# A LoRA residual kernel: one level of a seven-product matrix scheme against two levels, with another order of VectorE's queue

## The chip, the cores and the metric

The kernel runs on one core of a Trainium2 chip. The metric is the device time of one execution in microseconds (us), the median of three runs; what follows also reads one execution that the hardware profiler recorded.

## The reference, cut to what matters

Each of the two steps adds to x what a low-rank pair makes of it; the second also adds the product with a full matrix. x is (8, 512, 2048), W is (2048, 2048), every rank is 16, and all of it is float32.

```python
# step 1: A, B picked per batch element by itok_B_3_7
x = x + einsum('bnr,bor->bno', einsum('bni,bri->bnr', x, B[ids0]), A[ids0])
# step 2: lora_A, lora_B picked per batch element by itok_B_0_15
x = x + (einsum('bsi,io->bso', x, W)
         + einsum('bsr,bro->bso', einsum('bsi,bir->bsr', x, lora_A[ids1]), lora_B[ids1]))
```

## The kernel before, in words

The output is held transposed. The residual is put into the weights (W plus the identity, in the code `eye`), so that one matrix product gives nearly all, and the low-rank parts join it as one more matmul for each output tile: `in_mm` finds the values (`lr_ps`), `p_mm` finds the first step's A times W (`p_ps`), `join` makes `val`, `lr_out` adds `lr_w` times `val`.

A float32 operand is split into a rounded part and a rest: ScalarE (ACT) casts the rounded part (`w_hi` L555, `b_hi` L566), VectorE (DVE) subtracts it (`w_lo` L708, `b_lo` L721), and TensorE (PE) runs three matmuls for each tile: hi by hi, hi by lo, lo by hi (L1024).

The matrix product is done for pairs of batch elements by a seven-product scheme on 2x2 blocks of 1024 (`P1, P2, P6, P7, P4, P3, P5`), so 7 block products take the place of 8. A pair p has 7 products, each product 8 units, and a unit n is 4 output tiles by 2 chunks of 128 by 3 matmuls: 24 matmuls of 512 columns. The four pairs make 224 units. The sums of W's blocks are made once (`w_add` L694) and kept in HBM (`w_sum`), those of x are made in place (`t1` to `t4`).

Each engine has its own queue, written out by hand in the order of the units: in iteration n ACT and DVE split the operands of unit n + 1 into one of two buffers, PE works on unit n, and DVE adds the accumulator banks of ended tiles to what is kept (`add` L760 to L769, `add_last` L776 and L777). Five banks rotate (`BANKS`), and PE waits for the one of five tiles ago before it opens a new one:

```python
                    if j == 0 and k >= BANKS:
                        pe.wait_ge(*bank_free(k - BANKS))
```

A tile stays open over four units, and the adds of a group of four tiles are spread over the next ones. The SP queue issues the loads of W and x and the stores of W's sums, the POOL queue issues the loads picked by index, those of `lrw` and all stores of outputs.

Of the kernel before, what the change touches and what calls it, by code (L numbers as in the profile page):

```python
# [22 lines left out]
P1, P2, P6, P7, P4, P3, P5 = range(7)  # L24
PRODUCTS, UNITS = 7, 8

X11, X12, X21, X22 = range(4)

S2, S3 = range(2)

A11, A12, A21, A22 = range(4)

P_PRODUCTS = (P1, P2, P7, P4)


def lora_residual_program(nc, xT, ids0, ids1, A0n, B0, W, A1, B1, yT):
# [3 lines left out]
    N = xT.shape[3]  # L40
    D = C * P
    HC = C // 2
    HD = D // 2
    PAIRS = NB // 2
    LAST = PAIRS * PRODUCTS * UNITS
    BANKS, RAWS, STAGES = 5, 4, 4

    def at(n):
        return n // (PRODUCTS * UNITS), n // UNITS % PRODUCTS, n % UNITS

    def unit(p, o, u):
        return (p * PRODUCTS + o) * UNITS + u

    def diagonal(p, o, u):

        return (o in (P1, P4, P5) or (p, o) == (0, P6)) and u // 4 == u % 4 // 2

    def two_blocks(p, o):

        return o in (P3, P5) or (p, o) == (0, P6)  # L60
# [3 lines left out]
    raw_of, raw_plan = {}, []  # L64
    for n in range(LAST):
        p, o, u = at(n)
        raw_of[n] = len(raw_plan)
        raw_plan.append(n)
        if two_blocks(p, o) or (p, o) == (0, P1):
            raw_plan.append(n)  # L70

    def main_raw(n):
        return raw_of[n] % RAWS

    def second_raw(n):
        return (raw_of[n] + 1) % RAWS


    s3_stores, stores = {}, [0] * RAWS
    for u in range(UNITS):  # L80
        r = raw_of[u] + 1
        stores[r % RAWS] += 1
        s3_stores[r] = stores[r % RAWS]

    presums = [n for n in range(LAST) if two_blocks(*at(n)[:2]) or diagonal(*at(n))]
    begun = [n for n in presums if two_blocks(*at(n)[:2]) and diagonal(*at(n))]


    stage_plan = []
    for p in range(PAIRS):  # L90
        stage_plan += [("fix", p, q) for q in range(2 * UNITS)] if p == 1 else []
        for kind, half in (("c11", 0), ("c21", 1)):
            for g in range(2):
                stage_plan += [(kind, p, 4 * g + t) for t in range(4)]
                stage_plan += [("pst", half, g)] if p == 0 else []
    stage_at = {use: s for s, use in enumerate(stage_plan)}


    lr_plan = [(0, 1, 0, unit(0, P3, 2)), (0, 1, 1, unit(0, P3, 5)), (0, 0, 0, unit(0, P5, 5)),
               (0, 0, 1, unit(1, P1, 2))]  # L100
    for p in range(1, PAIRS):
        lr_plan += [(p, 0, 0, unit(p, P1, 5)), (p, 0, 1, unit(p, P7, 6)), (p, 1, 0, unit(p, P3, 2)),
                    (p, 1, 1, unit(p, P3, 5))]
    lr_index = {use[:3]: i for i, use in enumerate(lr_plan)}
    lr_split_at = {use[3]: i for i, use in enumerate(lr_plan)}
    lr_load_at = {use[3] - (2 if i == 4 or use[1:3] == (1, 0) else 3): i for i, use in enumerate(lr_plan)}


    join_at = {unit(p, P2, 2) if p else unit(0, P4, 1): 2 * p for p in range(PAIRS)}
    join_at |= {unit(p, P3, 2): 2 * p + 1 for p in range(PAIRS)}  # L110
    j_split_at = {unit(p, P2, 0) if p else unit(0, P4, 0): 2 * p for p in range(PAIRS)}
# [7 lines left out]
    stk_at |= {unit(p, P6, 6): (2 * p + 1, 0) for p in range(PAIRS)}  # L119
    stk_at |= {unit(p, P7, 5): (2 * p + 1, 1) for p in range(PAIRS)}  # L120

    def slot_due(n):

        if n < UNITS:
            if n + 1 < 4:
                return 0, n + 1
# [15 lines left out]
    def finds_p(n):  # L142
        return n // UNITS in P_PRODUCTS

# [944 lines left out]
```

## Time and profile before

| | |
|---|---|
| median of 3 runs | 1402.17 us (1401.36 to 1405.29) |
| the profiled execution's own time | 1402.34 us |
| its span, first to last instruction | 1400.7 us |
| PE busy | 1367.2 us (98%), 6016 matmuls |
| DVE busy | 810.2 us (58%) |
| ACT busy | 405.9 us (29%) |
| POOL busy | 165.0 us (12%) |
| DMA | 261.81 MB, mean 187 GB/s |

How to read it: busy is the time in which an engine had at least one instruction running, issues of transfers not counted. The profiled execution is a run like the others, and its own time is 1.6 us above its span, so that a sum made against the span needs 1.6 us to be a time.

### The profile page before, as it was taken

Reading aid. Unit: us, or ns where it says so; the run is one execution under the profiler, and the core shown is the slowest. Engines: PE = TensorE matmul, PEld = TensorE weight load, DVE = VectorE, ACT = ScalarE, POOL = GpSimd, SP = SyncE. Lnnn points to the kernel's source line nnn. Section 1 sums busy time; section 2 is a strip of 40 time slices with the busy share of each in tenths; the row PEclk is TensorE's granted clock in tenths of the full one; section 3 lists DMA queues with packets and bytes.
Section 4 is the critical chain, followed back from the end, with each engine's and each line's share of the span. In section 5 each row is a group of like instructions: output and inputs, shape, how many; then the busy total and the mean of one; then the engine's idle time right before and its main releaser. Section 6 shows DMA issues by size and latency. Waiting matters only on the chain.

```text
span 1400.7 us, 15653 instructions
## 1 busy us (share of the span) xinstructions
PE 1367.2 (98%) x6016; PEld 1129.2 (81%) x6016; DVE 810.2 (58%) x941; ACT 405.9 (29%) x462; POOL 165.0 (12%) x317
## 2 busy tenths in 40 slices
PE   5999999999999999999999999999999999999997
PEld 4888888888878888888887888888887888888886
DVE  3455855357776455646775555555766445554675
ACT  2332222223234223322332323232322422232230
POOL 3200100111123010012011010012012001001202
PEclk8999999999999999999999999999999999999999
DMA  8864843458887343357684252446785334234755
GB/s 303 310 225 134 299 158 113 153 186 280 294 280 240 122 136 120 129 195 246 236 289 146 86 173 96 151 151 213 256 297 187 99 120 135 91 91 133 223 201 180
DMA packets 76778, 261.81 MB, mean 187 GB/s; under 512 B 12176, under 2 KB 12176, under 8 KB 76576
## 3 DMA queue, kind: packets, MB, share of 16 engines
q1 hardware_dynamic: 57600, 205.55, 43.5%
q0 software_dynamic: 19104, 55.27, 11.7%
q8 instruction: 48, 0.79, 0.2%
q14 instruction: 26, 0.21, 0.0%
HBM read 213.52 MB, written 48.30 MB: 187 GB/s over the span
## 4 chain that ended last, share of the span: by engine, by line
PE 85%; DVE 5%; DMA 5%; ACT 2%; issue 2%; POOL 0%; POOLq 0%; SPq 0%; ACTq 0%; DVEq 0%
PE y_ps L1024 76%; PE lr_ps L955 4%; PE p_ps L997 3%; DMA w_raw<-in_W 2%; PE y_ps L976 2%; ACT w_hi L555 2%; DVE w_lo L708 1%; DVE w_raw L694 1%; DVE b_lo L721 1%; DMA w_raw<-w_sum 1%; DVE u L776 1%; DMA stage_all<-lrw 0%; DMA u<-in_A0n 0%; DVE u L777 0%; DVE val L835 0%
## 5 line engine op out<-in xcount | busy, mean ns | idle before, releaser
L1024 PE MATMUL y_ps<-b_hi,w_hi 128*128 128x512 f32 x1792 | 699.3, 390 | 15.3 <-DVE w_lo L708 8.8
L1024 PE MATMUL y_ps<-b_lo,w_hi 128*128 128x512 f32 x1792 | 698.6, 390 | 0.0
L1024 PE MATMUL y_ps<-b_hi,w_lo 128*128 128x512 f32 x1792 | 698.4, 390 | 0.0
L708 DVE TENSOR_TENSOR w_lo<-w_raw,w_hi 128x1024 fp32r<-128x1024 f32 x216 | 264.6, 1225 | 460.9 <-ACT w_hi L555 460.9
L555 ACT CAST w_hi<-w_raw 128x1024 fp32r<-128x1024 f32 x216 | 227.6, 1054 | 879.5 <-PE y_ps L1024 474.9
L1024 PEld LDWEIGHTS y_ps<-b_hi,w_hi 128*128 128x128 f32 x1792 | 337.3, 188 | 86.6 <-DVE w_lo L708 8.8
L1024 PEld LDWEIGHTS y_ps<-b_hi,w_lo 128*128 128x128 f32 x1792 | 337.2, 188 | 70.2
L1024 PEld LDWEIGHTS y_ps<-b_lo,w_hi 128*128 128x128 f32 x1792 | 337.3, 188 | 70.1
L721 DVE TENSOR_TENSOR b_lo<-x_raw,b_hi 128x1024 fp32r<-128x1024 f32 x112 | 136.5, 1219 | 0.0
L566 ACT CAST b_hi<-x_raw 128x1024 fp32r<-128x1024 f32 x112 | 117.5, 1049 | 2.4 <-DMA x_raw<-in_xT 2.4
L694 DVE TENSOR_TENSOR w_raw<-w_raw 128x1024 f32<-128x1024 f32 x64 | 78.1, 1221 | 19.5 <-DMA w_raw<-in_W 11.6
L377 POOL DMA_DIRECT2D out_y<-stage_all x64 | 34.9, 546 | 413.9 <-DVE stage_all L760 377.9
L760 DVE TENSOR_TENSOR stage_all<-y_ps,u 128x512 f32<-128x512 f32 x64 | 43.1, 688 | 20.8 <-PE y_ps L976 16.9
L955 PE MATMUL lr_ps<-b_hi,in_stk 128*128 128x512 f32 x128 | 50.4, 394 | 0.0
L955 PE MATMUL lr_ps<-b_lo,in_stk 128*128 128x512 f32 x128 | 50.3, 393 | 0.0
L381 POOL DMA_DIRECT2D out_y<-u x32 | 17.6, 548 | 260.1 <-DVE u L776 259.5
L769 DVE TENSOR_TENSOR u<-y_ps,u 128x512 f32<-128x512 f32 x64 | 41.1, 685 | 7.4 <-PE y_ps L1024 5.0
L976 PE MATMUL y_ps<-val,lr_w 128*128 128x512 f32 x112 | 44.0, 393 | 1.3 <-DVE val L835 1.1
L327 POOL DMA_DIRECT2D in_raw<-in_B x8 | 4.5, 563 | 307.6 <-issue 307.6
L341 POOL DMA_DIRECT2D lr_raw<-lrw x64 | 31.4, 497 | 76.1 <-DVE lr_w L817 68.6
L997 PE MATMUL p_ps<-w_hi,a_hi 128*128 128x512 f32 x64 | 26.0, 407 | 8.2 <-DVE a_lo L784 8.2
L955 PEld LDWEIGHTS lr_ps<-b_hi,in_stk 128*128 128x128 f32 x128 | 24.5, 191 | 5.2
(81 smaller groups left out, 605.8 us busy)
## 6 DMA issues: line engine op xcount, KB each, us to landing
w_raw<-in_W SPq DMA_DIRECT2D x208, 512.0 KB, 3.8
w_raw<-w_sum SPq DMA_DIRECT2D x96, 512.0 KB, 3.6
x_raw<-in_xT SPq DMA_DIRECT2D x64, 512.0 KB, 5.4
out_y<-u POOLq DMA_DIRECT2D x64, 256.0 KB, 6.4
out_y<-stage_all POOLq DMA_DIRECT2D x64, 256.0 KB, 3.4
lr_raw<-lrw POOLq DMA_DIRECT2D x64, 128.0 KB, 4.0
w_sum<-w_raw SPq DMA_DIRECT2D x8, 512.0 KB, 6.2
c_kept<-stage_all POOLq DMA_DIRECT2D x16, 256.0 KB, 3.2
```

Source lines behind the costliest of these rows:

```text
L377: pool.dma_start(dst, stage[s % STAGES][:, :]).then_inc(stage_stored[s % STAGES], 16)
L555: act.copy(w_hi[n % 2][:, :, :], w_tile(n)[:, :, :]).then_inc(w_hi_done, 1)
L566: act.copy(b_hi[:, 2 * j:2 * j + 2, :], x_raw[i][:, 2 * j:2 * j + 2, :]).then_inc(x_hi_done, 1)
L694: last = dve.tensor_tensor(raw[:, :, :], w_raw[main_raw(n)][:, :, :], w_raw[r % RAWS][:, :, :], ALU.subtract if o == P3 else ALU.add)
L708: dve.tensor_tensor(w_lo[n % 2][:, :, :], w_tile(n)[:, :, :], w_hi[n % 2][:, :, :].bitcast(F32), ALU.subtract).then_inc(w_ready, 1)
L721: dve.tensor_tensor(b_lo[:, 2 * j:2 * j + 2, :], x_raw[i][:, 2 * j:2 * j + 2, :], b_hi[:, 2 * j:2 * j + 2, :].bitcast(F32), ALU.subtract). ...
L760: dve.tensor_tensor(stage[s % STAGES][:, :], bank[:, :], (u2 if o == P2 else u3)[:, m, :], ALU.add).then_inc(added, 1)
L769: dve.tensor_tensor(u2[:, m, :], bank[:, :], u2[:, m, :], ALU.add).then_inc(added, 1)
L955: last = pe.matmul(lr_ps[:, :], cols, x[:, c, :], start=(first and c == 0 and x is b_hi), stop=(half == 1 and c == HC - 1 and x is b_lo))
L976: return pe.matmul(out[:, :], lr_w[i % 2][:, m * P:(m + 1) * P], val[b][:, :], start=start, stop=True)
L997: last = pe.matmul(p_ps[:, :], a0[:, 2 * j + c, :], w[n % 2][:, c, :], start=(j == 0 and c == 0 and k == 0), stop=(j == 3 and c == 1 and k ...
L1024: last = pe.matmul(bank[:, :], w[n % 2][:, c, t * P:(t + 1) * P], x[:, 2 * j + c, :], start=(j == 0 and c == 0 and w is w_hi and x is b_hi ...
```

## The change

The scheme is applied twice. Four batch elements (a "quad" k, two of them) are worked on together, an outer scheme of seven products `mo` (`M1, M2, M6, M7, M4, M3, M5`) on blocks of 1024, and inside each an inner scheme of seven products `po` (`Q1, Q2, Q6, Q5, Q7, Q3, Q4`) on blocks of 512. A quad has 49 products of 2 units each (`UNITS = 14` units for each mo), a unit is 2 output tiles by 4 chunks by 3 matmuls: again 24 matmuls of 512 columns. There are 196 units.

The inner products Q1, Q6, Q7 and Q4 (`CHAIN`) accumulate one on top of the other in four banks. The other three (Q2, Q5, Q3) go through a ring of two banks, `r_ps`. DVE adds every product to one or two targets as `ADDS` says; in M1 and M5 ACT copies the first of each target. The sums of operands: `t1` to `t4` (x) and, in the first quad alone, `s1` to `s4` (W) at the inner level, 128x2048 elements each; `xq` and `wq` at the outer level, from two operands, of which the second comes through a ring of three tiles `tmp` of 512 KB (`TMPS = 3`); `t3p` and `s3p`, whose two operands both come through `tmp` and whose result is stored to HBM from there. Outer partial results are kept in `u2` and in `stage`, stored and loaded again (`u3`). The second quad loads W's 49 operands ready-made. In it, tiles whose low-rank part was not known in time are loaded, seeded into a bank by ACT, given a matmul, and copied out (`fixes`, 48 units of M1 to M3), and eight further ones get theirs in `fin`.

Units and what falls in them (u is the unit within an outer product): Q1 u 0, 1; Q2 u 2, 3; Q6 u 4, 5; Q5 u 6, 7; Q7 u 8, 9; Q3 u 10, 11; Q4 u 12, 13. `s3p` (M1 of the first quad) and `t3p` (M2 of both) have one sum in each of u 5 to 12. The 8 gathers of one `a0` or `a1` tile also go through `tmp`.

The diff, cut to its core:

```diff
+CHAIN = (Q1, Q6, Q7, Q4)
+ADDS = {Q1: ((C11, True),), Q2: ((C11, False),), Q6: ((C12, True),), Q5: ((C12, False), (C22, True)),
+        Q7: ((C22, False),), Q3: ((C12, False),), Q4: ((C21, True),)}
-    BANKS, RAWS, STAGES = 5, 4, 4
+    LAST = QUADS * PRODUCTS * 2
+    TMPS = 3
...
+    def early_sums(n):
+        if u == 0 and x_worked(mo):
+            out.append(("xq", k, mo, 1))
+        if u == 4:
+            out.append(("t1", k, mo))
+        if u == 5 and k == 0:
+            out.append(("s1", mo))
+    def late_sums(n):
+            if u == 8 and x_worked(nmo):
+                out.append(("xq", nk, nmo, 0))
...
+        if u == 1:
+            out.append(("t2", k, mo))
+        if u == 2:
+            out.append(("t4", k, mo))
+        if k == 0:
+            if u == 1:
+                out.append(("s2", mo))
+            if u == 3:
+                out.append(("s4", mo))
+            if mo == M1 and 5 <= u < 13:
+                out.append(("s3p", *divmod(u - 5, 2)))
+        if mo == M2 and 5 <= u < 13:
+            out.append(("t3p", k, (C11, C12, C22, C21)[(u - 5) // 2], (u - 5) % 2))
...
+        # POOL
+            def load_tmp(e):
+                if e >= TMPS:
+                    pool.wait_ge(*tmp_free(tmp_plan[e - TMPS]))
...
+            def store_kept(kind, *key):
+                s, _ = tmp_stores[kind + "a", *key]
+                pool.wait_ge(kept_summed, kept_no[kind, *key])
...
+                    if kind in ("s3pb", "t3pb"):
+                        store_kept(kind[:3], *key)
+                        after = [e - 1, e]
+                    for f in after:
+                        if f + TMPS < len(tmp_plan):
+                            load_tmp(f + TMPS)
...
+        # ACT
+            def w_split(n):
+                q, h = divmod(n, 2)
+                if n >= 2:
+                    wait(unit_free(n - 2))
+                act.wait_ge(*w_is_there(q, h))
+                act.copy(w_hi[:, h, :, :], wq[w_tile(q)][:, h, :, :]).then_inc(w_hi_done, 1)
...
+        # DVE
+            for n in range(LAST + 2):
+                sums(early_sums(n))
+                if n + 1 < LAST:
+                    w_split(n + 1)
+                if n // 2 + 1 < LAST // 2:
+                    x_split(n // 2 + 1, n % 2)
+                for q, t, count, c, first in evicts(n, 0):
+                    if not by_act(q, first):
+                        evict(q, t, count, c, first)
...
+                for q, t, count, c, first in evicts(n, 1):
+                    if not by_act(q, first):
+                        evict(q, t, count, c, first)
+                if finish(n):
+                    fin(*finish(n))
+                sums(late_sums(n))
...
+                for key in a_splits(n):
+                    a_split(*key)
...
+        # PE
+                    if po in CHAIN:
+                        out = ps[:, t, :]
+                        if q:
+                            last_q = q - 7 + Q4 if po == Q1 else 7 * (q // 7) + CHAIN[CHAIN.index(po) - 1]
+                            pe.wait_ge(*a_free(last_q, h))
                     else:
+                        r = r_at["tile", q, t]
+                        out = r_ps[r % 2]
+                        if r >= 2:
+                            for pair in r_free(r - 2):
+                                pe.wait_ge(*pair)
...
+                    if n in fixes:
+                        fix(n, t % 2)
+                    if low:
+                        fin(*low, 1 - t % 2)
```

Here `evicts(n, 0)` names what is added of unit n - 1 (both banks of a chained product, the second tile of a ring product), and `evicts(n, 1)` the first tile of unit n, for ring products alone. `r_free` is the end of the adds that read the ring's bank two tiles earlier; `unit_free(n - 2)` is the end of unit n - 2 on PE; `tmp_free` is the end of the sum that used the tile, or, for a tile stored from, the landing of its store. The loads and stores of `tmp` are all issued by POOL, one after the other. In `fin` of the second quad DVE makes two sums of 128x1024, PE two matmuls, DVE two adds, PE two matmuls that wait for these adds, and DVE two adds.

## Rows read from the trace of the kernel before

**Rows 1.** The page's head: busy time of PE and DVE, the slices, the transfers.
```profile
PE 1367.2 (98%) x6016; PEld 1129.2 (81%) x6016; DVE 810.2 (58%) x941; ACT 405.9 (29%) x462; POOL 165.0 (12%) x317
PE   5999999999999999999999999999999999999997
PEclk8999999999999999999999999999999999999999
DMA packets 76778, 261.81 MB, mean 187 GB/s; under 512 B 12176, under 2 KB 12176, under 8 KB 76576
```
**Rows 2.** The page's chain of work that ended last, shares of the span by engine.
```profile
PE 85%; DVE 5%; DMA 5%; ACT 2%; issue 2%; POOL 0%; POOLq 0%; SPq 0%; ACTq 0%; DVEq 0%
```
**Rows 3.** Groups of instructions by line and shape: busy us, mean ns; idle before.
```profile
L1024 PE MATMUL y_ps<-b_hi,w_hi 128*128 128x512 f32 x1792 | 699.3, 390 | 15.3 <-DVE w_lo L708 8.8 <-DVE u L777 6.4
...
L708 DVE TENSOR_TENSOR w_lo<-w_raw,w_hi 128x1024 fp32r<-128x1024 f32 x216 | 264.6, 1225 | 460.9 <-ACT w_hi L555 460.9
L555 ACT CAST w_hi<-w_raw 128x1024 fp32r<-128x1024 f32 x216 | 227.6, 1054 | 879.5 <-PE y_ps L1024 474.9 <-PE p_ps L997 134.2 <-DVE w_raw L703 133.2
...
L760 DVE TENSOR_TENSOR stage_all<-y_ps,u 128x512 f32<-128x512 f32 x64 | 43.1, 688 | 20.8 <-PE y_ps L976 16.9 <-PE y_ps L1024 2.6
...
L573 ACT COPY u<-y_ps 128x512 f32<-128x512 f32 x32 | 18.7, 587 | 21.6 <-PE y_ps L1024 21.6
```
**Rows 4.** Timeline, 700 to 706 us: start, duration, engine, line, operation.
```profile
700.32 0.39 PE L1024 MATMUL y_ps<-b_hi,w_hi 128*128 128x512 f32 x1
...
702.71 1.05 ACT L555 CAST w_hi<-w_raw 128x1024 fp32r<-128x1024 f32 x1 [4.39 <-DVE w_raw L694]
...
703.79 1.23 DVE L708 TENSOR_TENSOR w_lo<-w_raw,w_hi 128x1024 fp32r<-128x1024 f32 x1 [1.17 <-ACT w_hi L555]
...
704.63 0.39 PE L1024 MATMUL y_ps<-b_hi,w_hi 128*128 128x512 f32 x1
...
704.94 0.68 DVE L776 TENSOR_TENSOR u<-y_ps,u 128x512 f32<-128x512 f32 x1
...
705.54 0.68 DVE L777 TENSOR_TENSOR u<-y_ps,u 128x512 f32<-128x512 f32 x1
```
**Rows 5.** Timeline, 58 to 60.5 us: weight loads of 128-column matmuls, a unit's end.
```profile
58.25 0.19 PEld L1005 LDWEIGHTS j_ps<-lr_w,a_lo 128*128 128x128 f32 x1
...
58.58 0.19 PEld L1005 LDWEIGHTS j_ps<-lr_w,a_lo 128*128 128x128 f32 x1
...
60.19 0.40 PE L1024 MATMUL y_ps<-b_hi,w_hi 128*128 128x512 f32 x1
...
60.39 1.05 ACT L555 CAST w_hi<-w_raw 128x1024 fp32r<-128x1024 f32 x1 [6.87 <-PE p_ps L997]
```
**Rows 6.** The tile w_sum's transfers of 512 KB, from issue to landing.
```profile
DMA to landing us min/median/max: 3.0/3.9/9.0
```
**Rows 7.** DMA issues, 0 to 70 us: count, KB each, median us to landing.
```profile
DMA packets 6237, 21.46 MB, mean 307 GB/s; under 512 B 1136, under 2 KB 1136, under 8 KB 6105
...
w_raw<-in_W SPq DMA_DIRECT2D x17, 512.0 KB, 5.9
...
w_sum<-w_raw SPq DMA_DIRECT2D x7, 512.0 KB, 5.5
```
**Rows 8.** Timeline of POOL, first and last of the 8 gathers of A.
```profile
9.10 0.59 POOL L389 DMA_DIRECT2D u<-in_A0n  x1 [6.25 <-issue]
...
17.54 0.54 POOL L389 DMA_DIRECT2D u<-in_A0n  x1 [0.59 <-issue]
```
**Rows 9.** The first matmul, and the first matmul behind the gathers, in the timeline.
```profile
8.84 0.80 PE L1024 MATMUL y_ps<-b_hi,w_hi 128*128 128x512 f32 x1 [8.84 <-DVE w_lo L708]
...
24.67 0.79 PE L997 MATMUL p_ps<-w_hi,a_hi 128*128 128x512 f32 x1 [8.20 <-DVE a_lo L784]
```
**Rows 10.** Windows: PE, PEld, DVE, ACT, POOL busy, PEclk, DMA share, GB/s.
```profile
16.00:24.60 8.60, 0.47 (x3) 0.05 (x1) 1.28 (x7) 0.85 (x3) 3.77 (x7) 0.72 0.86 300
...
24.60:30.00 5.40, 5.33 (x13) 4.17 (x14) 3.54 (x7) 2.83 (x5) 2.15 (x4) 0.50 0.66 187
```

More of the change, by code:

```diff
@@ L85, in lora_residual_program @@
[L85 to L95, printed above, removed]
@@ L106, in lora_residual_program @@
[L106 to L111, printed above, removed]
-    j_split_at |= {unit(p, P3, 0): 2 * p + 1 for p in range(PAIRS)}
-    j_load_at = {unit(p, P1, 3) if p else unit(0, P7, 4): 2 * p for p in range(PAIRS)}
@@ new lines, in product, with by_act @@
+    def product(q):
+        return q // 49, q // 7 % 7, q % 7
+    def by_act(q, first):
+        return first and product(q)[1] in (M1, M5)
+    fixes = {}
+    for mo, pair, own, quarters in ((M1, 0, 0, (0, 1)), (M2, 0, 0, (2, 3)), (M6, 1, 0, (0, 1)), (M7, 1, 0, (2, 3)),
+                                    (M4, 0, 1, (0, 1)), (M3, 0, 1, (2, 3))):
+        for i, u in enumerate((3, 4, 6, 7, 9, 10, 12, 13)):
+            fixes[unit(1, mo, u)] = (batch(own, pair, i // 2 % 2), 4 * quarters[i // 4] + 2 * (i % 2))
@@ new lines, in lora_residual_program, with use_tmp @@
+    lr_split_of = {i: n for n, uses in lr_split_at.items() for i in uses}
+    lr_mms = {}
+    for n in range(LAST + 1):
+        if n in fixes:
+            for t in range(2):
+                lr_mms["fix", n, t] = len(lr_mms) + 1
+        end = finish(n)
+        if end and end[0]:
+            for which in (1, 0):
+                for t in range(2):
+                    lr_mms["fin", end[1], end[2], which, t] = len(lr_mms) + 1
+    tmp_plan, tmp_when = [], []
+    def use_tmp(n, late, *key):
+        tmp_plan.append(key)
+        tmp_when.append((n, late))
@@ new lines, in lora_residual_program @@
+    g_at = {unit(0, M1, 5): 0, unit(0, M2, 5): 1}
+    p_no = {key: i + 1 for i, key in enumerate((mo, po) for mo in P_OF for po in P_Q)}
+    r_plan = []
+    for n in range(LAST):
+        if n % UNITS // 2 not in CHAIN:
+            r_plan += [("tile", n // 2, 2 * (n % 2)), ("tile", n // 2, 2 * (n % 2) + 1)]
+        if n in g_at:
+            r_plan.append(("g", g_at[n]))
+        if n in join_at:
+            r_plan.append(("join", *join_at[n]))
+    r_at = {key: r for r, key in enumerate(r_plan)}
@@ new lines, in lora_residual_program, with bank_of @@
+        p_reads, p_read = {}, {}
+        adds = copies = 0
+        for mo, po in p_no:
+            p_reads[mo, po] = {Q1: (0, 1), Q2: (0,)}.get(po, (1,))
+            if po == Q1 and mo in (M1, M4):
+                copies += 1
+                p_read[mo, po] = p_copied, copies
+            else:
+                adds += len(p_reads[mo, po])
+                p_read[mo, po] = p_added, adds
+        def bank_of(q, t, count):
+            if q % 7 in CHAIN:
+                return ps[:, t:t + count, :]
+            return r_ps[r_at["tile", q, t] % 2]
@@ L545, in _, with wait @@
+            for s in range(TMPS):
+                sp.wait_ge(tmp_stored[s], 16 * sum(stored_from(key) for key in tmp_plan[s::TMPS]))
+            for s in range(2):
+                sp.wait_ge(fix_stored[s], 16 * (len(fixes) // 2))
+            for c in range(4):
+                for h in range(2):
+                    sp.wait_ge(u2_stored[c][h], 16 * QUADS)
         @block.scalar
         def _(act):
+            def wait(pairs):
+                for pair in pairs:
+                    act.wait_ge(*pair)
@@ L943, in _ @@
+                if n in val_split_at:
+                    val_split(*val_split_at[n])
         @block.tensor
         def _(pe):
[L945 to L957 removed]
```

1951 lines of the change are left out of this document (1166 added, 785 removed).

## The prediction, made before the changed kernel ran

> **What bounds the kernel now.** I read the page's head first. PE is busy 1367.2 us of 1400.7, and from the second slice on every slice but the last is at nine tenths or more [rows 1]. The chain that ended last is PE for 85% [rows 2]. The groups then say that nothing starves it: 15.3 us of idle stand before 1792 of its matmuls, 8.8 of them at the start, while DVE waited 460.9 us for ACT's casts and those 474.9 us for PE [rows 3]. So the kernel is 6016 matmuls at their pitch. The timeline has that pitch: from 700.32 to 704.63 us is 19 matmuls, 0.227 us each [rows 4]; a unit of 24 is 5.44 us, a tile of 12 is 2.72. Times 6016 this is 1364 us.
>
> **What the change takes from PE.** The main product falls from 224 to 196 units, 5376 to 4704 matmuls. I count beside them 256 of in_mm, 128 of lr_out, 24 of join: 5112 matmuls at 0.227 = 1159 us. p_mm becomes 384 matmuls of 256 columns. No row has these. Below they can't beat 128 columns, whose weight loads come every 0.11 us (three from 58.25 to 58.58) [rows 5], above they don't exceed 0.227: 42 to 87 us. Half the columns lie near the lower end, I take 0.12, 46 us. With 48 matmuls of g at 0.11 (5 us) PE's work is 1210 us, 157 less than now. If all else were hidden, that would be the gain.
>
> **What it puts on DVE.** Issue to issue, a 128x1024 operation takes 1.15 us (703.79 to 704.94) and a 128x512 one from a bank 0.60 (704.94 to 705.54) [rows 4]; by this slope 1024 from a bank is 1.14 and the new 2048-element sums 2.2 (bounds: 2.1 to two of 1.15). For one outer product: 28 splits, 32 us; eight double-bank adds and sixteen single ones, 9 + 10; t1 to t4, 9; in the first quad s1 to s4, 9 more. That is 60 us, 69 in the first quad, before the outer sums, and 14 units are 76 us of PE. The outer sums (24 xq, 12 wq, 24 kept sums, 16 fins) add about 170 us in all. DVE goes to some 1100 us busy. It is no bound by its sum, but it now stands in line with PE at four places.
>
> **First place, the ring of two banks.** The second tile of a ring product's second unit needs the bank of that product's tile two before, which DVE adds in this same unit and behind both splits. From the unit's start: ACT begins 0.20 us later (60.19 to 60.39) [rows 5], casts 1.05, DVE follows at 1.29, splits w (1.15) and x (1.15), so the add starts at 3.58 and is complete 0.68 later: PE gets the bank at 4.3, and wanted it at 2.72. 1.6 us are lost after Q3, 2.2 after Q5 where two adds read each bank. In Q2 DVE arrives late, since t2 and t4 (and s2) stand in units 1 and 2. Walking DVE's queue by these durations through the 14 units: t2 ends 6.9 us into unit 1, so DVE comes 1.5 us late to unit 2, ends it at 7.8 and is 2.1 late to unit 3, whose second tile then waits 2.4. The waits come to 0.3 + 2.4 (Q2), 0.6 + 1.6 (Q5, half regained in front) and 1.6 (Q3) = 6.4 us for an outer product, 8.6 in the first quad, where s2 makes the first of them 2.4. ACT's seeds and copies of the fix units (0.59 each [rows 3], two in front of the cast) add about 1 in the second quad. p_mm and in_mm give DVE time and take some off. I carry for the seven, in order M1, M2, M6, M7, M4, M3, M5: 5, 5, 14, 9, 8, 10, 12 in the first quad (M6, M3 and M5 also have xq and wq at their edges) and 7, 4, 9, 8, 8, 8, 8 in the second. Sum 115. Without the cover of those extra matmuls it would be some 20 more.
>
> **In the last M5** fin's second pair of matmuls waits for DVE's adds of the first: splits to 3.6, adds of banks to 4.8, two sums to 7.2, two adds to 8.5, two matmuls to about 8.8, where the unit wants 6.3. Eight units at 2.6 are 21 us.
>
> **Second place, the ring of three tiles.** A kept sum reads two tiles; the next but three load may be issued only when the store from the first has landed, and DVE waits for it in its one queue, with the split of the unit after next behind. One turn is the sum 1.22, the store, the load, and 0.2 for the handover. A 512 KB transfer of w_sum lands in 3.9 us median, 3.0 at least [rows 6]: a turn is 9.2 us (7.4 at least), PE's own pace 5.44 to 8.6. Where two operands of xq or wq come between (u 8 to 12 of M2; u 8, 10, 12 in the second quad), another sum and load are in the turn: 9.2 + 1.3 + 3.9 = 14.4. From u 5 to u 12: M1 seven turns, 64 us, for 48 that PE would take (with its p_mm, in_mm and ring waits), +16. M2 2 x 9.2 + 5 x 14.4 = 90, +42. M2 of the second quad 4 x 9.2 + 3 x 14.4 = 80 for 49, +31. Sum 89. At the least landing it is near 45.
>
> **Third place, the gathers through the same ring.** Eight gathers take POOL 9.0 us to issue (9.10 to 18.1) [rows 8], and the tile lands some 4 later. In M7 at u 12 two such tiles stand ahead of a0's split, the second issued only after xq's tile is free, about 6.5 us into the unit: 6.5 + 13 + the difference and both splits 3.5 = 23, and the split for the next product but one comes 2.4 after, where PE wants it at 10.9: +15. At M5's start, with one, +11. Handovers of xq and wq tiles at the edges of M6, M4 and M5: +15, a guess between 0 and 30. Sum 41.
>
> **Ends.** The first matmul comes at 8.84 now [rows 9]; two 1 MB operands and four more identity adds make that about 12.5, and p_mm still waits for the gathers, as it does now (24.67 [rows 9]), after which the clock is at half, 1.2 GHz, for some us (0.50 from 24.6 to 30.0) [rows 10]. I take 20 us over the work for the start, and 8 for the last fin and its stores.
>
> **Sum.** 1210 + 115 + 21 + 89 + 41 + 20 + 8 = 1504 us of span, + 1.6 outside it = 1505. The profiled execution (1402.34) is the median (1402.17) within 0.2 us, so this stands against either: 7% slower. 0.3% is about what a measurement of this kernel can tell from no change.
>
> **The rivals.**
> Transfers slow down under their own load. I count 399 MB where there were 262: the 173 tiles of the ring 91, x 59, W 81, stores of W's sums 44, other stores and the fixes 124. In M2 some 44 MB move. In the first 70 us of the trace, at 307 GB/s, 512 KB loads took 5.9 us and stores 5.5 [rows 7]. Turns are then 12.8 and 20.0 us, the third sum 180 instead of 89, the total 1596. For it: M2 needs 300 GB/s at my own forecast. Against: the load is this dense only in M1 and M2.
>
> The clock falls. After 8.2 us of idle [rows 9] the clock went to half, 1.2 GHz (0.50) [rows 10]. If the waits of M1's and M2's kept sums do this each time, a unit's 24 matmuls take up to twice 5.44 us, about one short turn, and where p_mm or a bank wait comes on top it runs over: some 2 us on each of 24 units, +45 in all, 1550. Against: most of my waits are 1.6 to 5 us; PEclk is 9 in every slice after the first [rows 1], though PE has hardly a wait there. The Trainium skill (TensorE: Matmul & The Clock Gate, "HAM oscillation") describes a kernel that waits for a transfer between groups of matmuls and runs each group at the low clock. By that rule it would be 1550; no row here has such a pattern.
>
> The three-tile ring does not hold DVE, because landings are near 3 us and POOL has issued ahead. Then the kept sums and handovers cost nothing, only bank waits, gathers and ends remain: 1505 - 89 - 15 = 1401, no change. To be faster, the gathers' tiles must also have come early (26 less), 1375. It decides from a turn under about 6.9 us, PE's mean pace there, that is two landings under 5.5 together; the least of the rows gives 6.0 [rows 6].
>
> The change does what its matmul count says, all else hidden: 1240. Against it stands the bank wait, made of three durations that hardly vary.
>
> **Chances.** The forecast, 1450 to 1560: 0.5. Slow transfers or low clock, 1560 to 1660: 0.22. Ring mostly hidden, 1406 to 1450: 0.12; fully, within 0.3% of 1402: 0.03; faster with the gathers hidden too: 0.10; all hidden: 0.03. So faster 0.13, same 0.03, slower 0.84. The range 1390 to 1600 leaves about 0.11 below it (half of the cases near 1375 and all hidden, with a little) and 0.08 above; the slower cases alone hold 1430 to 1600.
>
> **What the profile of the changed kernel would show.** PE's busy near 1210 to 1240 us, DVE's near 1100. PE idle before ring tiles released by DVE's adds, 1.5 to 2.5 us, some 40 times. In M2 (about 150 to 290 us, and again about 140 us long in the second quad) units spaced 9 and 14 us, DVE idle at the kept sums, released by transfers into tmp; the clock there says which rival. One hole of about 15 us at the end of M7. The prediction is wrong if the tmp transfers are not what DVE waits for in M2, if the landing there is far from 3.9, or if the matmul pitch is not 0.227. DMA should total 400 MB.

## The result, and the profile after

The changed kernel takes 1705.34 us (median of 4 runs, 1698.28 to 1710.05) where the one before took 1401.76: the ratio is 1.2156, its 95% interval 1.2101 to 1.2212. It is 21.6% slower; 7% was forecast, and the time lies above the range. The profiled execution took 1698.28 us, its span is 1696.6.

The page of the changed kernel, the lines that answer to [rows 1] and [rows 2]:

```profile
PE 1328.5 (78%) x5544; PEld 1057.9 (62%) x5544; DVE 1114.0 (66%) x1105; ACT 570.4 (34%) x720; POOL 346.6 (20%) x603
...
PE   5879673469996998966897897457898888888895
...
PEclk9989896779998999987998998778999999999998
...
DMA packets 106324, 401.25 MB, mean 236 GB/s; under 512 B 15092, under 2 KB 15092, under 8 KB 99716
...
PE 26%; issue 23%; DMA 20%; DVE 20%; POOL 4%; ACT 3%; POOLq 1%; DVEq 0%; ACTq 0%
```

The reader is to see that the work is as counted (5544 matmuls, 401 MB, DVE 1114 us busy) and that the kernel has no bound of its own any more. PE had 85% of the chain that ended last [rows 2] and has 26%; transfers and DVE have 20% each. "issue", time for which the profile shows no wait, has 23% where it had 2%. Part of it hides waits for transfers: one such piece runs from 233.78 to 242.77 us, and DVE waited for a load of the three-tile ring in 8.83 us of the same stretch (its line stands below). Two valleys stand in PE's row, deepest in the seventh and eighth slice and in the 26th and 27th: M2 of either quad. The granted clock has its 6 and three of its five 7s there too.

Groups of the changed kernel, as in [rows 3], and its transfers from issue to landing:

```profile
L1636 PE MATMUL ps<-b_hi,w_hi 128*128 128x512 f32 x1568 | 650.8, 415 | 258.0 <-DVE stage L1380 108.9
...
L1349 DVE TENSOR_TENSOR w_lo<-wq,w_hi 128x1024 fp32r<-128x1024 f32 x196 | 239.8, 1224 | 317.9 <-ACT w_hi L1069 317.2
...
L1310 DVE TENSOR_TENSOR xq<-xq 128x2048 f32<-128x2048 f32 x56 | 127.8, 2283 | 0.0
L1161 ACT COPY ps<-wq 128x512 f32<-128x512 f32 x96 | 56.7, 590 | 195.9 <-DMA wq<-c_kept 190.4
...
tmp<-t_kept POOLq DMA_DIRECT2D x48, 512.0 KB, 6.5
wq<-c_kept POOLq DMA_DIRECT2D x48, 512.0 KB, 7.1
out_y<-wq POOLq DMA_DIRECT2D x48, 512.0 KB, 4.7
```

258 us of idle stand before PE's first matmuls of a chunk, where 15.3 stood [rows 3], most of it (109 + 66 us in the view of waits below) released by DVE's adds. ACT's seeds of the fix units waited 190.4 us for their loads. The loads of the three-tile ring land in 6.5 us, not in the 3.9 of [rows 6].

From the starts of the splits of w (one a unit, L1349) the length of each outer product can be read. Beside the changed kernel stand four of the runs below. "Forecast" is worked out from the prediction's terms, to about 3 us: PE's work in that product and the waits that it put there. The first M1 has none, since the start of the kernel lies in it, and the second M5 is left out.

| product | forecast | changed | adds first | no kept x sums | no fix copies | five out |
|---|---|---|---|---|---|---|
| first M1 | | 134.7 | 135.6 | 134.8 | 135.5 | 98.4 |
| first M2 | 142 | 174.6 | 179.1 | 113.6 | 173.6 | 112.2 |
| first M6 | 90 | 114.5 | 107.3 | 113.3 | 115.4 | 104.8 |
| first M7 | 108 | 109.4 | 98.5 | 109.9 | 109.3 | 92.2 |
| first M4 | 96 | 94.1 | 88.5 | 94.0 | 94.3 | 90.6 |
| first M3 | 94 | 105.0 | 100.3 | 105.3 | 105.5 | 99.3 |
| first M5 | 111 | 124.6 | 117.8 | 123.7 | 124.6 | 112.5 |
| second M1 | 94 | 114.6 | 110.9 | 115.8 | 104.7 | 106.0 |
| second M2 | 122 | 158.5 | 156.3 | 108.7 | 153.9 | 86.2 |
| second M6 | 89 | 106.4 | 99.5 | 104.6 | 97.5 | 93.8 |
| second M7 | 95 | 109.0 | 99.5 | 108.3 | 95.3 | 87.0 |
| second M4 | 88 | 104.8 | 95.2 | 101.5 | 87.0 | 81.3 |
| second M3 | 95 | 104.0 | 98.1 | 105.5 | 92.7 | 87.0 |

### The profile page after: what moved, and what is told of

Read it like the earlier page. It is cut to its first block, busy times and chain, and to the rows that moved or that the text cites. A ratio compares the mean times of both kernels' runs of the same rounds, so it can differ in the third digit from the quotient of the medians.

```text
span 1696.6 us, 16085 instructions
## 1 busy us (share of the span) xinstructions
PE 1328.5 (78%) x5544; PEld 1057.9 (62%) x5544; DVE 1114.0 (66%) x1105; ACT 570.4 (34%) x720; POOL 346.6 (20%) x603
## 4 chain that ended last, share of the span: by engine, by line
PE 26%; issue 23%; DMA 20%; DVE 20%; POOL 4%; ACT 3%; POOLq 1%; DVEq 0%; ACTq 0%
PE ps L1636 22%; DMA wq<-c_kept 5%; DVE w_lo L1349 4%; DVE xq L1310 3%; DMA tmp<-in_W 3%; DVE stage L1380 3%; DVE b_lo L1355 3%; DMA tmp<-in_xT 2%; DMA t_kept<-tmp 2%; ACT w_hi L1069 2%; DMA tmp<-t_kept 2%; POOL tmp L790 2%; DMA out_y<-wq 1%; PE ps L1603 1%; PE ps L1566 1%
## 5 line engine op out<-in xcount | busy, mean ns | idle before, releaser
L1636 PE MATMUL ps<-b_hi,w_hi 128*128 128x512 f32 x1568 | 650.8, 415 | 258.0 <-DVE stage L1380 108.9
L1636 PE MATMUL ps<-b_lo,w_hi 128*128 128x512 f32 x1568 | 638.6, 407 | 0.0
L1636 PE MATMUL ps<-b_hi,w_lo 128*128 128x512 f32 x1568 | 636.4, 406 | 0.0
L1636 PEld LDWEIGHTS ps<-b_hi,w_hi 128*128 128x128 f32 x1568 | 312.5, 199 | 357.0 <-issue 143.0
L1349 DVE TENSOR_TENSOR w_lo<-wq,w_hi 128x1024 fp32r<-128x1024 f32 x196 | 239.8, 1224 | 317.9 <-ACT w_hi L1069 317.2
L1069 ACT CAST w_hi<-wq 128x1024 fp32r<-128x1024 f32 x196 | 205.7, 1049 | 533.7 <-PE ps L1636 379.2
L1636 PEld LDWEIGHTS ps<-b_hi,w_lo 128*128 128x128 f32 x1568 | 310.9, 198 | 69.7
L1636 PEld LDWEIGHTS ps<-b_lo,w_hi 128*128 128x128 f32 x1568 | 312.6, 199 | 63.8
L1355 DVE TENSOR_TENSOR b_lo<-xq,b_hi 128x1024 fp32r<-128x1024 f32 x196 | 238.9, 1219 | 4.1 <-ACT b_hi L1075 3.8
L1075 ACT CAST b_hi<-xq 128x1024 fp32r<-128x1024 f32 x196 | 205.3, 1048 | 88.1 <-DVE xq L1295 63.8
L1310 DVE TENSOR_TENSOR xq<-xq 128x2048 f32<-128x2048 f32 x56 | 127.8, 2283 | 0.0
L1161 ACT COPY ps<-wq 128x512 f32<-128x512 f32 x96 | 56.7, 590 | 195.9 <-DMA wq<-c_kept 190.4
L1318 DVE TENSOR_TENSOR tmp<-tmp 128x1024 f32<-128x1024 f32 x24 | 29.4, 1225 | 119.7 <-DMA tmp<-in_xT 82.7
L1531 PE MATMUL ps<-val,lr_w 128*128 128x512 f32 x128 | 56.9, 458 | 61.3 <-ACT ps L1161 50.4
L1380 DVE TENSOR_TENSOR u<-ps,u 128x512 f32<-128x512 f32 (+1 forms) x124 | 100.3, 839 | 2.3 <-PE ps L1636 2.1
L872 POOL DMA_DIRECT2D out_y<-wq x48 | 34.9, 727 | 210.2 <-ACT wq L1165 190.6
```

The lines of the kernel that those rows point to most:

```text
L1069: act.copy(w_hi[:, h, :, :], wq[w_tile(q)][:, h, :, :]).then_inc(w_hi_done, 1)
L1075: act.copy(b_hi[:, 2 * (q % 2) + j, :, :], xq[x_use(q)[0]][:, j, :, :]).then_inc(x_hi_done, 1)
L1161: act.copy(p_ps, fix_tile[fix_no[n] % 2][:, t, :]).then_inc(seeded, 1)
L1310: dve.tensor_tensor(xq[dst][:, :, :, :], xq[a][:, :, :, :], xq[b][:, :, :, :], ALU.subtract).then_inc(x_summed, 1)
L1349: dve.tensor_tensor(w_lo[:, h, :, :], wq[w_tile(q)][:, h, :, :], w_hi[:, h, :, :].bitcast(F32), ALU.subtract).then_inc(w_ready, 1)
L1355: dve.tensor_tensor(b_lo[:, slot, :, :], xq[x_use(q)[0]][:, j, :, :], b_hi[:, slot, :, :].bitcast(F32), ALU.subtract).then_inc(x_ready, 1)
```

## The experiments

Sixteen kernels ran. Each comes from the changed kernel by the edit shown; differences are to its 1705.34 us. Its own four runs spread over 12 us, and most of the others have two runs, so a single difference under 10 us says little. Some of the edits leave out needed work or read other data than they should; they show what a place costs and are no kernels to use.

### The place of the adds in DVE's queue

```diff
             for n in range(LAST + 2):
                 sums(early_sums(n))
+                for q, t, count, c, first in evicts(n, 0):
+                    if not by_act(q, first):
+                        evict(q, t, count, c, first)
                 if n + 1 < LAST:
                     w_split(n + 1)
                 if n // 2 + 1 < LAST // 2:
                     x_split(n // 2 + 1, n % 2)
-                for q, t, count, c, first in evicts(n, 0):
-                    if not by_act(q, first):
-                        evict(q, t, count, c, first)
```

> DVE adds the banks of the ended unit ahead of the splits, as the kernel's two-level form would without the second half of the change; all else as changed (1705 us). If the ring of two banks costs what I worked out (1.6 to 2.4 us at the second tile of each of 42 ring products, where nothing else holds the unit), the banks are free before PE asks and some 40 to 75 us go: 1630 to 1665 us. If the adds' place is nothing because DVE waits for transfers anyway, it stays within 10 us of 1705. If the later splits starve PE instead, it is over 1715.

1624.82 us (ratio to the kernel before 1.1619, interval 1.1564 to 1.1673): 80 us less, where 40 to 75 were expected. PE's waits for DVE's adds halve; the same rows of the view of waits (us in total, times, longest), in the changed kernel and in this run:

```profile
PE ps L1636 <- DVE stage L1380: 108.9, 37, 18.0
PE ps L1636 <- DVE u L1380: 66.0, 26, 10.5
...
PE ps L1636 <- DVE stage L1380: 48.4, 9, 15.1
PE ps L1636 <- DVE u L1380: 42.1, 11, 15.4
```

63 waits became 20, where the forecast had some 40; 59 of the 63 stood in the second unit of a ring product. Against it, PE's waits for w_lo grew from 7.1 to 62.5 us, nearly all in the first quad. One wait can be seen in the last units of the first M6. In the changed kernel, the timeline of PE and of DVE:

```profile
423.39 0.39 PE L1636 MATMUL ps<-b_hi,w_lo 128*128 128x512 f32 x1
424.99 0.50 PE L1636 MATMUL ps<-b_hi,w_hi 128*128 128x512 f32 x1 [1.21 <-DVE u L1380]
```

```profile
421.97 1.23 DVE L1349 TENSOR_TENSOR w_lo<-wq,w_hi 128x1024 fp32r<-128x1024 f32 x1 [1.34 <-ACT w_hi L1069]
423.11 1.22 DVE L1355 TENSOR_TENSOR b_lo<-xq,b_hi 128x1024 fp32r<-128x1024 f32 x1
424.25 1.28 DVE L1380 TENSOR_TENSOR u<-ps,u 128x512 f32<-128x512 f32 x2
```

DVE waits for ACT's cast, splits w and x, and adds the bank at 424.25; PE asked for it at 423.6 and opens the tile at 424.99. The same unit with the adds first (it runs at other times there):

```profile
421.34 0.69 DVE L1380 TENSOR_TENSOR u<-ps,u 128x512 f32<-128x512 f32 x1 [1.35 <-PE ps L1636]
...
422.43 1.23 DVE L1349 TENSOR_TENSOR w_lo<-wq,w_hi 128x1024 fp32r<-128x1024 f32 x1 [0.40 <-ACT w_hi L1069]
```

The add falls into the time in which DVE waits for the cast, starts 3 us earlier with respect to the unit, and pushes the split back by nothing. In that order PE has no wait in this stretch.

### The kept sums and their ring of three tiles

Left out the sums of x:

```diff
-        if mo == M2 and 5 <= u < 13:
-            out.append(("t3p", k, (C11, C12, C22, C21)[(u - 5) // 2], (u - 5) % 2))
...
-                        pool.wait_ge(*kept_store("t3p", k, c, j))
-                        src = t3_kept[c, :, j, :, :]
+                        src = xT[batch(k, 1, c % 2), c // 2, :, j, :, :]
```

> Leaves out the 16 kept sums of x in M2 of both quads with their 32 loads and 16 stores; what reads their result loads a block of x of the same size instead. If the ring of three tiles is what M2 waits for (174.6 and 158.5 us between its first splits and the next product's), M2 falls to about 120 and 112 and the total by 95 to 110 us, to about 1600. If M2's length comes from something else (clock, all transfers together), it falls by less than 50.

1586.56 us, 119 less, somewhat more than the 95 to 110 expected: M2 from 174.6 and 158.5 to 113.6 and 108.7, and no more than 3.3 us in any other product. The edit takes away 32 loads and 16 stores as well as the sums, so it gives the price of the place and not of one link in it.

The same for W in the first M1:

```diff
-            if mo == M1 and 5 <= u < 13:
-                out.append(("s3p", *divmod(u - 5, 2)))
...
-                        pool.wait_ge(*kept_store("s3p", c, h))
-                        src = w_kept_at(M7, c)[:, h, :, :]
+                        src = W[4 * (c // 2) + c % 2, :, h, :, :]
```

> Leaves out the 8 kept sums of W in M1 of the first quad; what reads their result loads a block of W instead. By the same ring theory M1's units from u 7 on (9 to 14 us) fall to 6 to 9 and the product from 134.7 us to about 108: total 1675 to 1685. If M1 is long from its start (gathers, clock, first loads), under 10 us go.

1671.19 us, 34 less (its two runs lie 12 us apart), M1 from 134.7 to 109.5. One turn in M2 shows where the time is. The timeline of the changed kernel, DVE and POOL (L1318 is the kept sum, L1246 the sum of wq with its second operand from the ring):

```profile
241.26 1.23 DVE L1318 TENSOR_TENSOR tmp<-tmp 128x1024 f32<-128x1024 f32 x1 [8.83 <-DMA tmp<-in_xT]
...
242.78 0.54 POOL L866 DMA_DIRECT2D t_kept<-tmp  x1 [9.00 <-DVE tmp L1318]
...
245.97 0.53 POOL L790 DMA_DIRECT2D tmp<-w_ops  x1 [2.66 <-DMA t_kept<-tmp]
...
252.82 1.23 DVE L1246 TENSOR_TENSOR wq<-wq,tmp 128x1024 f32<-128x1024 f32 x1 [5.80 <-DMA tmp<-w_ops]
254.08 0.90 DVE L1224 TENSOR_TENSOR wq<-wq,eye 128x128 f32<-128x128 f32 x4
...
255.28 0.55 POOL L790 DMA_DIRECT2D tmp<-in_xT  x1 [7.52 <-DVE wq L1224]
...
261.44 1.23 DVE L1318 TENSOR_TENSOR tmp<-tmp 128x1024 f32<-128x1024 f32 x1 [6.46 <-DMA tmp<-in_xT]
```

From sum to sum it is 20.2 us: the sum and its handover 1.5, the store 3.2, a load 6.8, the sum of wq with the identity 2.5, the next load 6.2. These are the prediction's links; it had 14.4, with 3.9 for each landing and 1.3 for the sum of wq. The two loads took 5.2 us more than that, the sum with the identity 1.2 more, and the store 0.7 less.

The landing goes with what else is under way. Over the changed kernel, 512 KB loads took 4.0 us in the median where no other transfer of 256 KB or more was in flight at their issue (42 loads), 5.8 with two of them (108), 6.8 with three (124) and 9.1 with five (31). In the kernel before it was 3.5 with none (136 loads) and 6.2 with three (41).

Next, the loads of both operands in 256 of their 1024 columns:

```diff
+                cols = 256 if kind in ("t3pa", "t3pb") else 1024
-                pool.dma_start(tmp[slot][:, :, :].rearrange("p s n -> p (s n)"), ...
+                pool.dma_start(tmp[slot][:, :, :].rearrange("p s n -> p (s n)")[:, 0:cols], ...
```

> The two operands of each kept sum of x are loaded in 256 of 1024 columns (the rest is what the tile held); the sum, the store and the order of the ring are as before. If a turn of the ring is the landing of its serial loads, the operand's 6.2 us falls to 3 or so and M2's long units from 15 to 20 us to 12 to 17, the total by 30 to 50 us. If the landing is a wait for POOL's issue or a latency that does not go with size, under 15 us.

1676.51 us, 29 less, just under the 30 to 50 expected; M2 fell by 12.6 and 8.5 us. A quarter of the bytes did not bring a quarter of the landing. The issues in 222 to 310 us of that run, and behind them the same loads in the same window of the changed kernel:

```profile
tmp<-in_xT POOLq DMA_DIRECT2D x10, 128.0 KB, 5.2
...
tmp<-w POOLq DMA_DIRECT2D x2, 512.0 KB, 6.3
...
tmp<-in_xT POOLq DMA_DIRECT2D x9, 512.0 KB, 6.3
```

Last, the second quad's kept sums of x moved from M2 to M1:

```diff
-        if mo == M2 and 5 <= u < 13:
+        if mo == (M1 if k else M2) and 5 <= u < 13:
             out.append(("t3p", ...
```

> In the second quad the kept sums of x stand in M1's units 5 to 12, where no xq sum stands between them, instead of M2's. If a turn with two operands of xq in it costs two landings in a row and one without costs one, M2 of the second quad falls from 158.5 to about 112 and M1 rises from 114.6 to 130 to 140: total 20 to 35 us less. If only the amount of transfers counts, the total stays within 10 us of 1705.

1683.40 us, 22 less. Second M2 158.5 to 111.1, second M1 114.6 to 149.0: a turn without an operand of xq in it is shorter, by less than I had expected, since M1's eight sums cost 34 us and not 20.

### The fix units

Left out the loads into the two tiles, ACT's seeds and copies, and PE's wait for them; POOL moves the tile from HBM to HBM instead:

```diff
         # PE
-                pe.wait_ge(seeded, 2 * fix_no[n] + t + 1)
-                lr_out(b, m + t, p_ps, False)
+                lr_out(b, m + t, p_ps, True)
         # POOL
...
-                pool.dma_start(fix_tile[f % 2], c_kept[b * C + m:b * C + m + 2, :, :].rearrange("m p n -> p m n")
-                               ).then_inc(fix_loaded[f % 2], 16)
+                pool.dma_start(yT[b * C + m:b * C + m + 2, :, :], c_kept[b * C + m:b * C + m + 2, :, :]
+                               ).then_inc(fix_stored[f % 2], 16)
         # ACT: seed and fixed_copy left out; POOL: store_fix left out
```

> Leaves out the low-rank part of the 96 tiles of the fix units: no seed, no copy out by ACT, no load into a tile; POOL moves the tile from HBM to HBM, PE's matmul runs into its bank without waiting. If the fix units' load, seed, copy and store chain is the term that I mis-sized (second quad's products 9 to 20 us over my walk), 60 to 90 us go: 1615 to 1645. If, as I forecast, ACT's copies add only about 1 us a product, 5 to 15 us go.

1629.27 us, 76 less, all in the second quad: M1 to M3 lose 5 to 18 us each. The prediction had about 1 us a product for it. Is it that ACT's casts stand behind seeds which wait?

```diff
         # ACT, each iteration
-                if n - 1 in fixes:
-                    fixed_copy(n - 1, 1)
-                if n in fixes:
-                    seed(n, 0)
                 if 0 <= n < LAST:
                     if n + 1 < LAST:
                         w_split(n + 1)
...
+                if n - 1 in fixes:
+                    fixed_copy(n - 1, 1)
                 if n in fixes:
+                    seed(n, 0)
                     fixed_copy(n, 0)
                     seed(n, 1)
```

> ACT casts the next unit's operands ahead of the fix units' copy out and seed, instead of behind them. Leaving the whole chain out gave 76 us. If most of it is that the casts stand behind a seed that waits for its load, 25 to 60 us go: 1645 to 1680. If it is the loads' and stores' own turn (two tiles, a store and a load in a row for every three units), PE waits for the seed instead and under 15 us go.

1718.74 us, 13 more, where 25 to 60 less were expected if that were so. PE now waits for the seed instead; the waits of PE in that run:

```profile
PE ps L1530 <- ACT ps L1161: 92.5, 32, 9.5
```

In the changed kernel that row is 50.4 us. So I tried the turn of the two tiles:

```diff
-                pool.dma_start(fix_tile[f % 2], c_kept[b * C + m:b * C + m + 2, :, :].rearrange("m p n -> p m n")
+                pool.dma_start(fix_tile[f % 2][:, :, 0:128],
+                               c_kept[b * C + m:b * C + m + 2, :, 0:128].rearrange("m p n -> p m n")
```

> The fix tiles are loaded in 128 of each 512 columns (the rest is what the tile held); seeds, copies and stores as before. If the turn of the two fix tiles (copy, store 4.7 us, load 7.1 us, seed, matmul) is the 76 us, a load that lands in 3 to 4 us takes 25 to 60 us off: 1645 to 1680. If ACT's copies are the cost, under 10.

1678.89 us, 26 less. Here too a 128 KB load landed in 5.0 us where the full one took 7.1:

```profile
wq<-c_kept POOLq DMA_DIRECT2D x48, 128.0 KB, 5.0
```

Two microseconds off a landing gave 26 us back. So the loads are in the chain, which is the turn of two tiles (copy, store, load, seed, matmul), one for every three units. That this turn makes up the whole 76 us is read from the timeline and not shown by a run. There is one more link in it, POOL's queue: the load of a tile is issued behind the store of the other one. POOL and ACT in the second M6 of the changed kernel (L872 stores, L810 loads, L1161 seeds):

```profile
1205.36 0.73 POOL L872 DMA_DIRECT2D out_y<-wq  x1 [6.36 <-ACT wq L1165]
1214.76 0.72 POOL L872 DMA_DIRECT2D out_y<-wq  x1 [8.68 <-ACT wq L1165]
1215.47 0.71 POOL L810 DMA_DIRECT2D wq<-c_kept  x1
...
1222.58 0.59 ACT L1161 COPY ps<-wq 128x512 f32<-128x512 f32 x1 [6.22 <-DMA wq<-c_kept]
```

The first store landed 5.1 us after its issue, at 1210.5; the load into its tile went out at 1215.47, 5.0 us later. The seed of that load started at 1222.58, after ACT had waited 6.22 us with the next cast behind it. An earlier place for these loads in POOL's queue was not tried. From load to load a tile turned in 18 to 22 us once this product was under way, where three units of PE's work are 16.3.

### The gathers

```diff
-                for b in range(NB):
-                    a = id1(b) if which else id0(b)
-                    pool.dma_start(tmp[slot]...[:, b, :, :],
-                                   src[bass.ds(a, 1), :, kh * HC:(kh + 1) * HC, :].rearrange("a p c r -> (a p) c r")
-                                   ).then_inc(tmp_loaded[slot], 16)
+                pool.dma_start(tmp[slot][:, :, :].rearrange("p s n -> p (s n)")
+                               .rearrange("p (b m) -> p b m", b=NB),
+                               src[0:NB, :, kh * HC:(kh + 1) * HC, :].rearrange("a p c r -> p a (c r)")
+                               ).then_inc(tmp_loaded[slot], 128)
```

> The 8 gathers by index of each a0 or a1 tile become one load of 512 KB of the first eight adapters (so the adapters are not the ones asked for). If POOL's issue of 8 gathers in the three-tile ring is what holds M7's last unit (21.9 us) and M5's first two (15.9 and 19.9), these fall to 7 to 10 and the total by 30 to 40 us, to about 1670. If the wait there is the ring's order alone, under 10 us.

1687.88 us, 17 less, half of what was expected. M7's last unit went from 21.9 to 18.1 us, M5's second from 19.9 to 12.9; against it, the first split of w came at 15.8 us instead of 12.3. In M7 the second tile's one load is issued at 528.2 and its sum starts at 536.49, in the timeline of this run:

```profile
528.20 0.91 POOL L728 DMA_DIRECT2D tmp<-in_A0n  x1 [1.76 <-DVE xq L1293]
...
536.49 1.23 DVE L1416 TENSOR_TENSOR tmp<-tmp 128x1024 f32<-128x1024 f32 x1 [6.41 <-DMA tmp<-in_A0n]
```

The issue of eight gathers is only a part of that hole. By this reading the rest is the ring's order, which lets the load go only behind the sums of xq, and some 8 us to the sum.

### PE's own pace and the clock

Left out one of the three matmuls of each tile and chunk, hi by lo:

```diff
-                        for i, (w, b) in enumerate(((w_hi, b_hi), (w_hi, b_lo), (w_lo, b_hi))):
+                        for i, (w, b) in enumerate(((w_hi, b_hi), (w_lo, b_hi))):
...
```

> Leaves out the matmul hi by lo of every chunk, 1568 of the 4704 of the product (356 us of PE at full clock); the splits stay as they are. If PE's pace, half clock included, is what the changed kernel's units last, about 350 us go: 1350 or less. If the units are set by DVE's queue, the transfers and the two rings, less than half of it goes: 1500 to 1600, and M2 stays within 10 us of 174.6 and 158.5 us.

1646.67 us: 356 us of matmuls at full clock were taken away, PE's busy time fell by 267.5 us (the granted clock was 0.83 over that run, 0.91 over the changed kernel), and the kernel lost 59. M2 is 180.2 and 160.3 us long, no shorter than before. That answers the rival of the clock for M2. M2 of the first quad, one window of the changed kernel (columns as in [rows 10]), and PE's timeline at the end of one of its waits:

```profile
147.00:322.00 175.00, 109.92 (x504) 90.19 (x502) 95.83 (x95) 33.72 (x37) 39.48 (x72) 0.83 0.72 244
```

```profile
267.41 0.77 PE L1636 MATMUL ps<-b_hi,w_hi 128*128 128x512 f32 x1 [18.01 <-DVE stage L1380]
...
270.11 0.46 PE L1636 MATMUL ps<-b_hi,w_hi 128*128 128x512 f32 x1
```

The granted clock was 0.83 there, about a third of the stretch at 1.2 GHz. The Trainium skill (TensorE: Matmul & The Clock Gate, "HAM oscillation") describes how such waits for a transfer lower the clock, and the trace agrees. But it costs little here: the low stretch around this wait began at 253.2 us and ended at 270.3, PE stood still until 267.41, and six matmuls took 2.70 us where they take 1.36 at full clock. Over the whole kernel 317 us stand at 1.2 GHz and PE is busy in 166 of them; at 427 ns from matmul to matmul against 227, that is about 80 us of busy time more than at full clock. By this run's slope, 59 for 267.5, it would be worth somewhat under 20 us of the kernel's time, an estimate.

### DVE's sums, and val's split

```diff
-                dve.tensor_tensor(wq[2][:, :, :, :], wq[2][:, :, :, :], wq[0][:, :, :, :], ALU.subtract
+                dve.tensor_tensor(wq[2][:, :, :, 0:8], wq[2][:, :, :, 0:8], wq[0][:, :, :, 0:8], ALU.subtract
... the same in s2 and s4
```

> Leaves out most of three of W's four inner sums (s2, s3, s4 on 8 of each 256 columns), 21 DVE operations of 2.28 us, 44 us of DVE in the first quad; their stores stay. By my walk the sums cost the bank waits of Q2 and Q3 about 2 us a product, 15 us in all: 1680 to 1695. If the first quad is bound by DVE's work, 35 us or more go. If by transfers, under 5.

1694.01 us, 11 less for 43 us of DVE's busy time: little beside the spread, in line with the prediction's walk through DVE's queue, and far from the 35 or more that a bound by DVE's sum of work would give.

```diff
         # DVE
+                if n in val_split_at:
+                    val_split(*val_split_at[n])
                 sums(late_sums(n))
...
-                if n in val_split_at:
-                    val_split(*val_split_at[n])
```

> DVE splits val ahead of the late sums of its unit instead of behind them. The joins stand in the ring of two banks, and in M6 unit 3 is 15.5 and 14.9 us long behind them. If the ring waits for val's split there, these units fall by 3 to 5 us each, as after M5's first, and 8 to 20 us go: 1685 to 1697. If PE waits there for something else, under 4 us.

1706.81 us, no change; this gives nothing alone, whatever M6's long unit is made of.

### Sums of edits, and whole kernels

These four put together edits that are shown above, as their expectations list them.

> The three edits at once: adds ahead of the splits, no kept sums of x, no seeds and copies in the fix units. Each alone gave -80, -119 and -76 us. If the three places are separate stretches of the span, the sum holds: 1705 - 275 = 1430, at most 20 off. If they share waits (a unit that waits for one of them does not pay for the other), it ends at 1460 to 1490.

1431.38 us against 1430 from the sum: the adds' place, the kept sums of x and the fix units' chain are separate stretches.

> Adds first, kept sums of x and of W left out, fix units' seeds and copies left out, gathers as one plain load. Single effects: -80, -119, -34, -76, -17. If all are separate stretches: 1705 - 326 = 1379. If what is left of the first quad is DVE's queue with its sums, and covers part of them, 1390 to 1410.

1390.04 us (ratio to the kernel before 0.9916, interval 0.9889 to 0.9944), 11 more than the sum. So five places (the adds' order, and four that this run clears only by leaving out needed work or by reading from another source) are the whole distance to the one-level kernel and 12 us beyond (under 1%). PE is busy 1252.6 of 1387.5 us in it:

```profile
PE 1252.6 (90%) x5544; PEld 1028.7 (74%) x5544; DVE 1084.5 (78%) x1073; ACT 468.3 (34%) x528; POOL 237.9 (17%) x434
```

> A whole kernel with the four reorderings at once: adds ahead of the splits, casts ahead of seeds, val's split ahead of the late sums, kept sums of x of the second quad in M1. If the places stay separate, as they were in the run with three left out, the sum of the single gains holds: 1705 - 80 - 22 and 20 to 80 more, 1525 to 1585. It stays slower than the one-level kernel, since M2 and M1 of the first quad keep their ring of three.

1649.19 us, where 1525 to 1585 were expected: slower than the adds' place alone, and 31 more than the sum of the four single effects (-80, -22, +13, +1). The next kernel is this one without the casts ahead of the seeds and without val's early split, and it takes 46 us less. The difference lies in the second quad's fix units: its M6 is 108.0 us here and 96.9 there, its M4 105.3 and 92.6. Val's split alone did nothing, so it is most likely the casts ahead of the seeds, which cost more once the adds are out of the way; these two edits were not tried apart on top of the others.

> A whole kernel with two reorderings: DVE adds the banks ahead of the splits, and the second quad's kept sums of x stand in M1. Alone they gave -80 and -22. Both, if separate: 1603, at most 8 off. If the adds' early place lengthens the turn of the three-tile ring, nearer 1625.

1603.24 us (ratio 1.1442, interval 1.1413 to 1.1471), the sum to the microsecond, and the best whole form of two levels found here. It is still 14% slower than the kernel before; no version that does all the work beats that one.

## Why the prediction was wrong, point by point

The direction and its mechanism held: the matmuls' gain of 157 us is real in the counts and is lost to waits at the two rings, the fix units, the gathers and the edges. The size was 193 us short by the profiled execution (a span of 1696.6 us against 1504) and 200 by the medians (1705 against 1505), to which the differences below belong. Two steps failed: the fix units' term and the landings in the ring of three tiles.

**PE's work** was right: 5544 matmuls, 0.227 us each at full clock, and 256 columns come every 0.12 us, the value taken between 0.11 and 0.227. The changed kernel's timeline, eleven steps from the first to the last:

```profile
556.66 0.28 PE L1603 MATMUL ps<-w_hi,lr_w 128*128 128x256 f32 x1
...
557.98 0.28 PE L1603 MATMUL ps<-w_hi,lr_w 128*128 128x256 f32 x1
```

**The ring of two banks**, 115 us: the mechanism is shown. Putting the adds first gave 80 back; the forecast 1.6 us for Q3 is 1.4 in the example above, and the new 2048-element sum took 2283 ns, 2.2 from issue to issue. What of the other 35 is there was not measured.

**The fix units** are the step that failed, "ACT's seeds and copies of the fix units add about 1 in the second quad". It took seeds as instructions and did not ask when their loads may be issued. The loads turn through two tiles, with a store's landing and another store's place in POOL's queue in each turn; the walk was made for the three-tile ring and not for this one. Leaving the chain out gave 76 us, against about 7. The load's landing is shown to be part of it (26 us for 2 us off each); how the other 50 divide among the links is open, but ACT's order alone is not it.

**The ring of three tiles** was right in its links and wrong in the landing of the loads: 3.9 us from [rows 6], a median over a kernel at 187 GB/s, where the loads of the turn above took 6.8 and 6.2. Its store took 3.2, less than the median of either row. 89 us were forecast and 153 measured (119 + 34). That the landing is far from 3.9 was one of the prediction's own signs of being wrong. The rival that went by [rows 7] had 180 for this term, too much because stores do not take 5.5 us there, and 1596 in total, since it lacked the fix units too.

**The gathers**, 26 us: at least 17 shown; M7's last unit measured 21.9 us, where the walk gives 15 over 5.4 and some in_mm. **M5's fins** were not tried. **The handovers** at the edges of M6, M4 and M5, 15 us: too small by reading alone. In the run with five out the units that stand out are M6's first and fourth (16.8 and 13.3 us), M5's first two (15.6 and 11.9), second M1's third (22.9, where lr_w's first loads come) and M7's last (17.3); six units of about 6 us would be some 60 shorter. They were not taken apart.

**The sum.** Of the 200 us missing, the fix units are 69 and the ring of three tiles 64. Some 20 are the clock by the estimate above. About 47 stay open, more if part of the 35 of the two-bank ring did not come; those edges are a guess at where.

**The ranking of the rivals.** "No change" and "faster" needed two landings under 5.5 us together; in the turn above they were 10.0. The clock gives next to nothing in M2. Transfers slowed by their own load was the case whose mechanism came, and 0.22 for it and the low clock together was too low: the very count of 399 MB that stood beside it speaks for loaded landings in M2, at 300 GB/s of my own forecast (244 were measured). Its band, 1560 to 1660, was missed too.

## What to carry to other kernels

A level of such a scheme trades matmuls for operands and partial results that pass through small rings. Count each ring's turn (use, store's landing, load's landing, and every instruction that holds the queue between), with landings from a stretch as dense as the new one, before counting what PE saves; and do this for every ring, the small ones too. In an in-order queue, what frees a buffer goes into the time in which the queue would wait anyway, here for the other engine's cast, and not behind the work that follows it.

## What the runs showed of the hardware that I had not expected

A load's landing went by its company more than by its size. With three other large transfers in flight at its issue, a 512 KB load took 6.8 us in the median, with none 4.0; a quarter of the bytes took off only 1.1 us in M2 (5.2 against 6.3) and 2.1 in the fix units (5.0 against 7.1).

Separate places add up closely: three edits gave 274 us together where their single effects sum to 275, and two gave their sum to the microsecond, in a kernel in which four engines and two queues wait for each other. It does not hold for every set of edits: four reorderings together ended 31 us above their sum.
